# A linear-attention and feed-forward layer: x's loads behind K's reads, the residual's bias on VectorE, one normalisation later on ScalarE

## The reference

```
q, k, v = x @ Wq.T + bq, x @ Wk.T + bk, x @ Wv.T + bv     # cut into heads
q, k    = exp(q), exp(k)
kv, k1  = cumsum over tokens of k (outer) v, cumsum over tokens of k
att     = (q . kv) / (q . k1)                             # per head and token
x1      = layernorm(x + att @ Wo.T + bo)
h       = x1 @ weight @ aux_weight1 @ aux_weight2
out     = layernorm(x1 + tanh(h + bias))
```

## Time and profile before

| | us |
|---|---|
| median of 3 runs | 2340.22 (2339.27 to 2342.91) |
| the profiled execution | 2341.11, of it the traced span 2339.2 |

### The profile page before, as it was taken

The page is one execution under the profiler, slowest core; times in us unless marked ns, Lnnn a source line. Parts: engine busy times, 40 slices in busy tenths (PEclk is TensorE's granted clock), DMA queues, the critical chain, the costliest instruction groups (busy, mean ns, idle before and its releaser), DMA issues.

```text
span 2339.2 us, 71230 instructions
## 1 busy us (share of the span) xinstructions
PE 2249.3 (96%) x27784; PEld 1834.5 (78%) x27784; DVE 1494.7 (64%) x2316; ACT 1004.2 (43%) x1683; POOL 1415.9 (61%) x1925
## 2 busy tenths in 40 slices
PE   3999999999999999999999999999999999999985
PEld 2778888888888888888888888888888888878863
DVE  3466676666666766666667666676676666666653
ACT  2344444444444444444444444444444444444432
POOL 1256666666666666666666666666666666666563
PEclk9999999999999999999999999999999999999997
DMA  5133333333333333333333333333333333333221
GB/s 155 48 96 112 107 109 111 103 110 109 106 113 100 113 110 101 110 109 106 113 101 110 114 100 113 106 108 111 103 110 111 101 114 105 107 108 101 71 67 50
DMA packets 294452, 242.73 MB, mean 104 GB/s; under 512 B 33328, under 2 KB 225840, under 8 KB 294192
## 3 DMA queue, kind: packets, MB, share of 16 engines
q1 hardware_dynamic: 294192, 238.69, 32.6%
HBM read 139.99 MB, written 98.57 MB: 102 GB/s over the span
## 4 chain that ended last, share of the span: by engine, by line
PE 92%; DVE 2%; issue 2%; SPq 1%; DMA 1%; ACT 1%; POOL 1%; POOLq 0%; DVEq 0%; ACTq 0%
PE SC L312 25%; PE SC L313 24%; PE SC L314 24%; PE SC L410 6%; PE ND L419 5%; PE ND L397 3%; PE ND L393 2%; PE ND L429 2%; DVE o L684 1%; SPq L277 1%; DMA xres<-x 0%; PE ND L312 0%; PE ND L314 0%; DVE WK L654 0%; PE ND L313 0%
## 5 line engine op out<-in xcount | busy, mean ns | idle before, releaser
L723 POOL TENSOR_SCALAR_AFFINE_SELECT A<-A 128x512 f32<-128x512 f32 x512 | 329.3, 678 | 297.3 <-ACT A L532 297.2
L684 DVE RECIPROCAL o<-ND 128x512 f32<-128x512 f32 x128 | 427.8, 3342 | 1.6 <-PE ND L419 1.3
L700 DVE TENSOR_TENSOR xres<-SC,xres 128x512 f32<-128x512 f32 x128 | 88.5, 692 | 483.2 <-PE SC L314 358.0
L734 POOL TENSOR_TENSOR oL<-o,oH 128x512 fp32r<-128x512 f32 x128 | 165.3, 1291 | 325.0 <-ACT oH L542 325.0
L522 ACT ACTIVATE WK<-xres,shift,rstd 128x512 f32<-128x512 f32 x128 | 104.1, 813 | 501.5 <-POOL shift L770 501.5
L532 ACT ACTIVATE A<-SC 128x512 f32<-128x512 f32 x512 | 264.3, 602 | 36.0 <-PE SC L410 35.0
L312 PE MATMUL SC<-xTH,WqH 128*128 128x512 f32 x512 | 211.1, 412 | 32.3 <-POOL xTL L761 27.6
L312 PE MATMUL SC<-WoH,oH 128*128 128x512 f32 x512 | 202.4, 395 | 17.8 <-issue 16.5
L761 POOL TENSOR_TENSOR xTL<-xin,xTH 128x512 fp32r<-128x512 f32 x128 | 165.6, 1294 | 85.9 <-ACT xTH L567 85.9
L654 DVE TENSOR_TENSOR_SCAN WK<-ones,k,KT 128x128 f32<-128x128 f32 x512 | 207.6, 467 | 8.8 <-PE ND L393 8.3
L312 PE MATMUL SC<-WfH,x1H 128*128 128x512 f32 x512 | 201.0, 393 | 10.4 <-POOL x1L L748 9.4
(11 more groups left out here) (100 smaller groups left out, 5006.0 us busy)
## 6 DMA issues: line engine op xcount, KB each, us to landing
xin<-x SPq DMA_DIRECT2D x512, 64.0 KB, 2.0
xres<-x SPq DMA_DIRECT2D x128, 256.0 KB, 2.6
x_rows<-WK SPq DMA_DIRECT2D x128, 256.0 KB, 2.6
WK<-x_rows SPq DMA_DIRECT2D x512, 64.0 KB, 1.9
out<-WK SPq DMA_DIRECT2D x128, 256.0 KB, 2.0
k_rows<-WK SPq DMA_DIRECT2D x120, 256.0 KB, 2.0
WK<-k_rows SPq DMA_DIRECT2D x480, 64.0 KB, 1.9
QT<-wqT SPq DMA_DIRECT2D x4, 256.0 KB, 4.8
```

The lines of the kernel that those rows point to most:

```text
L684: nc.vector.reciprocal(o[:, :, :], den_ps).then_inc(recip_ready, 1)
L723: last = nc.gpsimd.affine_select(out=A[:, k % 2, j, :, :], in_=A[:, k % 2, j, :, :], compare_op=ALU.is_ge, fill=0.0, base=0, pattern=[[0, ...
L734: nc.gpsimd.tensor_tensor(oL[:, :, :], o[:, :, :], oH[:, :, :].bitcast(F32), ALU.subtract).then_inc(ol_ready, 1)
```

## The change

It moves three steps and touches no buffer. On SyncE the four loads of x's tile k+9 go behind the reads of x1 and K. The residual's bias is added on VectorE, in the slot in which the sum is made and right ahead of it, and no longer on GpSimd a slot earlier. On ScalarE the result's normalisation goes behind V's copy and x's split.

```
@@ -269,13 +269,6 @@
                     n = k - 1
                     wait_before(sp, (k_turned, c.count(n + 1)))
                     sp.dma_start(k_rows, KS).then_inc(k_stored[n % B], 16)
-                if c.exists(k + 9):
-                    n = k + 9
-
-                    wait_before(sp, (xl_ready, c.count(n - 1)))
-                    for j in range(HG):
-                        sp.dma_start(xin[j * HD:(j + 1) * HD, n % XIN, :].rearrange("p (t f) -> p t f", t=HG),
-                                     x_b[n % B, c.it + n // B, j]).then_inc(xin_loaded[n % B], 16)
                 if c.exists(k - 2):
                     n = k - 2
 
@@ -289,6 +282,13 @@
                     for j in range(HG):
                         sp.dma_start(Ktok[j * HD:(j + 1) * HD, :].rearrange("p (a c) -> p a c", a=HG),
                                      k_blocks[j]).then_inc(ktok_loaded[n % B], 16)
+                if c.exists(k + 9):
+                    n = k + 9
+
+                    wait_before(sp, (xl_ready, c.count(n - 1)))
+                    for j in range(HG):
+                        sp.dma_start(xin[j * HD:(j + 1) * HD, n % XIN, :].rearrange("p (t f) -> p t f", t=HG),
+                                     x_b[n % B, c.it + n // B, j]).then_inc(xin_loaded[n % B], 16)
                 if c.exists(k):
                     if c.static() and c.it * B + k == 0:
                         sp.wait_ge(c_done, 1)
@@ -551,11 +551,6 @@
                     wait(act, k_turned, c.quad_count(k - 4))
                     nc.scalar.activation(KT[:, ns, b, :], kproj_ps, ACT.Exp,
                                          bias=bcol[:, 1, b:b + 1]).then_inc(k_ready, 1)
-                if fin:
-                    n = k - 3
-                    wait(act, shift2_ready, c.count(n + 1))
-                    nc.scalar.activation(y[:, n % 2, :], y[:, n % 2, :], ACT.Identity, bias=shift[:, 1:2],
-                                         scale=rstd[:, 1:2]).then_inc(out_ready, 1)
                 if att:
                     wait(act, v_done, c.count(k + 1))
                     wait(act, state_done, c.state_count(k - 1))
@@ -568,6 +563,11 @@
                         xTH[:, (k // QUAD) % 2, :, b * P:(b + 1) * P].rearrange("p g (t q) -> p g t q", q=HD),
                         xin[:, k % XIN, :].rearrange("p (t g q) -> p g t q", t=HG, q=HD),
                         ACT.Copy).then_inc(xh_ready, 1)
+                if fin:
+                    n = k - 3
+                    wait(act, shift2_ready, c.count(n + 1))
+                    nc.scalar.activation(y[:, n % 2, :], y[:, n % 2, :], ACT.Identity, bias=shift[:, 1:2],
+                                         scale=rstd[:, 1:2]).then_inc(out_ready, 1)
 
             run_slots(act, slot, 8, 3, {-7: split_wq, -5: split_wk, -4: split_aux, -3: split_a12,
                                         -2: split_wv_wf_wo, -1: free_staging})
@@ -695,6 +695,8 @@
                     wait(dve, x1s_loaded[n % B], c.part_count(n))
                     nc.vector.transpose(x1s[:, :], x1s[:, :]).then_inc(x1_turned, 1)
                 if prev:
+                    wait(dve, xres_loaded[(k - 1) % B], c.dma_count(k - 1))
+                    nc.vector.tensor_tensor(r, r, cbc[:, :], ALU.add).then_inc(xb_ready, 1)
                     wait(dve, oproj_done, c.count(k))
                     wait(dve, xb_ready, c.count(k))
                     nc.vector.tensor_tensor(r, oproj_ps, r, ALU.add).then_inc(r_ready, 1)
@@ -747,12 +749,6 @@
                     halves = [t[:, :, :].rearrange("p g (t q) -> p g t q", q=HD) for t in (x1H, x1L)]
                     nc.gpsimd.tensor_tensor(halves[1], x1s[:, :].rearrange("p (t g q) -> p g t q", t=HG, q=HD),
                                             halves[0].bitcast(F32), ALU.subtract).then_inc(x1l_ready, 1)
-                if att:
-                    if not prev:
-                        pool.wait_ge(c_ready, 1)
-                    wait(pool, xres_loaded[k], c.dma_count(k))
-                    nc.gpsimd.tensor_tensor(xres[:, k % 2, :], xres[:, k % 2, :], cbc[:, :],
-                                            ALU.add).then_inc(xb_ready, 1)
                 if c.exists(k + 8):
                     m = k + 8
                     xs, cols = (m // QUAD) % 2, slice(m % QUAD * P, (m % QUAD + 1) * P)
```

More of the change, by code:

```diff
@@ L271, in slot @@
                     sp.dma_start(k_rows, KS).then_inc(k_stored[n % B], 16)
[L272 to L278, removed]
                 if c.exists(k - 2):
@@ L553, in slot @@
                                          bias=bcol[:, 1, b:b + 1]).then_inc(k_ready, 1)
[L554 to L558, removed]
                 if att:
@@ L749, in slot @@
                                             halves[0].bitcast(F32), ALU.subtract).then_inc(x1l_ready, 1)
[L750 to L755, removed]
                 if c.exists(k + 8):
```

## The result

| | us |
|---|---|
| before | 2340.22 (2339.27 to 2342.91) |
| after, median of 5 runs | 2354.84 (2350.71 to 2359.99) |
| ratio | 1.006 [1.0047, 1.0073] |
| the profiled execution after | 2359.99, of it the traced span 2358.2 |

The forecast was 2337.7, in a range of 2334 to 2343. The kernel became slower by 14.6 us, and the forecast was wrong. The profiled execution is the slowest of the five; its span is 19.0 us longer than that of before, so what follows sizes about 19 us where the medians differ by 14.6.

What follows compares the result with a forecast made beforehand. TensorE was taken to bound the kernel, with 11.4 us of disturbances the most to gain. Gains of 0.9 us (SyncE's order) and 1.6 us (bias move), ScalarE's order 0, took 2340.22 to 2337.7 us, range 2334 to 2343.

Steps and rivals of the forecast that it cites:

- What bounds the kernel: TensorE bounds the steady stretch: undisturbed slots last 17.24 us, and all disturbances over 112 slots are 11.4 us.
- the unnamed 5 us of disturbances: TensorE, steady stretch: the remaining 5 us or so of 11.4 are later starts not counted as idle.
- Part 1: SyncE's order: reads of x1 start 3.1 us earlier in slot 53, L696's 1.34 us wait goes; gain at most 0.9 us.
- The gain of 0.9 us: TensorE's waits ahead of the feed-forward in slots 113 and 115 go, at most 0.41 and 0.5 us.
- rival A: Nothing arrives at TensorE: late slots had other causes too, or other slots become late instead; 2340.2 us, chance 0.25.
- Part 2: Residual's bias from GpSimd to VectorE: removes TensorE's waits for L532, gain 1.6 us; addition takes 0.69 us at cost 0.
- three waits for L532: TensorE's Q product waits three times for ScalarE's copy of the scores; all should go, 1.6 us.
- Part 3: ScalarE's order: V's copy and x's split no longer wait behind the normalisation, result's store up to 1.2 us later; worth 0.
- The sum: Whole kernel: 0.9 + 1.6 = 2.5 us gained, so a median of 2337.7 us.
- last sign: Forecast is wrong if an undisturbed slot isn't 17.24 us or disturbances over 112 slots grow beyond 11.4 us.
- D: SyncE's reads don't get earlier because x1's store lands later beside K's; 2338.6 us, chance 0.58 together with the forecast.
- C: VectorE's addition stops GpSimd for its whole length, x1L 0.14 us late in each of 112 slots; 2356 us, chance 0.07.

Runs made afterwards that it cites:

- e2: Kernel before with only SyncE's new order (x's loads behind the reads of x1 and K); 2347.57 us, ratio 1.0032.
- e4: Kernel before with SyncE's new order and the residual's bias on VectorE, ScalarE's order unchanged; 2344.19 us, ratio 1.0015.
- e10: Kernel before with SyncE's new order and the bias addition on VectorE right behind the quotient (L686), ScalarE's order unchanged; 2341.72 us, ratio 0.9996.
- e1: Kernel before with only ScalarE's new order (result's normalisation behind V's copy and x's split); 2342.92 us, ratio 1.0011.
- e11: Kernel before with ScalarE's new order and one needless one-column GpSimd instruction ahead of x1L, bias still on GpSimd; 2359.16 us, ratio 1.0064.
- e7: Kernel before with ScalarE's new order and the bias on VectorE, SyncE's order unchanged; 2354.70 us, ratio 1.0064.
- e9: Kernel after with the addition L699 moved directly behind the quotient L686, where GpSimd has nothing to do; 2345.88 us, ratio 1.0012.
- e12: Kernel of e9 with GpSimd's x1L ahead of the second normalisation's scale and shift; 2340.91 us, ratio 0.9994.
- e3: Kernel before with only the residual's bias moved from GpSimd to VectorE; 2344.47 us, ratio 1.0017.
- e6: Kernel after with the result's store issued a slot later, ahead of the residual's load; 2342.54 us, ratio 1.0013.

## Why the prediction was wrong

**What bounds the kernel** held: TensorE does, and an undisturbed slot is 17.24 us in both kernels. But I listed the L429 waits "with no releaser" and the unnamed 5 us of disturbances and didn't ask what they were. More than half of all the 11.4 us is waits for the program. In before, TensorE's starts that come over 0.13 us late add up to 10.3 us in slots 9 to 120; of these 6.5 us, in 17 places at L429, L313 and once L393, come 1.3 to 1.5 us after a block's landing. In after it is 27.8 of 29.6 us, counting distances of 1.1 to 1.8 us.

**Part 1** was right in its mechanism. In slot 53 of after the reads of x1 start 2.92 us behind its store. SyncE's timeline, to be read against the earlier trace rows:

```profile
1011.78 0.33 SPq L267 DMA_DIRECT2D x_rows<-WK  x1
1014.70 2.83 SPq L277 DMA_DIRECT2D WK<-x_rows  x4
1021.74 0.35 SPq L296 DMA_DIRECT2D xres<-x  x1
1024.30 0.37 SPq L300 DMA_DIRECT2D out<-WK  x1
```

VectorE's wait of L696 for `x_rows` fell from 98.0 us to 9.3. One statement failed, "The residual's load stays about where it was": in the median of a place in the loop pass it moved by up to 0.9 us in e2 and up to 1.3 us in after. That cost 0.32% in e2 and was free beside part 2 (e4). The gain of 0.9 us came where it was forecast: slots 113 and 115, 18.08 and 17.95 us before, are 17.24 in after. But slot 114, 17.24 before, takes 18.33 in after and 18.34 in e10, so it was taken back next door, as rival A had it. In e10, with both parts in a harmless form, the time can't tell (0.9996, with 2.5 us inside the interval).

**Part 2.** The gain is there in kind: GpSimd's L761 waits for VectorE's statistics nearly always, so that GpSimd is no longer the late one, and one of three waits for L532 is left (1.6 us before, 1.0 after). Waits of after, whole span:

```profile
POOL ve L761 <- DVE mv L706: 231.0, 127, 4.2
DVE WK L696 <- DMA WK<-x_rows: 9.3, 13, 2.7
```

The step that failed is "GpSimd's list can be stretched [...] x1L still comes 0.93 - 0.38 = 0.55 us early. Cost 0". The stretch was right in size: x1L came 0.33 us later, and in slot 63 still 0.73 us ahead of its product. What failed is that I measured its spare time at the product alone. The fetch of the next block of TensorE's program follows x1L too, and for that second user less than 0.3 us was to spare once the store was in the way (e1 against e11). The duration failed too: 0.69 us was taken for L699 between 0.69 and 1.07, and it took 1.146 on average, above both ends. The 1.07 us of slot 1 was no ceiling: there the product started with 0.53 us left of GpSimd's mask (L723) and ended 0.54 us after it. Beside oL 0.65 us were left, and the same 0.54 us on top give the longer time. The row to read was how much of GpSimd's work is left when the addition starts. VectorE's idle time covered that, as the text said: L702 still waits for TensorE, 3.51 us in slot 53 of after.

**Part 3** failed at "The result's store is issued up to about 1.2 us later [...] 0". It was 0.76 us later, and the only question put was who wants its buffer. Whose transfers it meets was not asked. Alone it cost 0.11% (e1), about as little as I said; together with the addition it cost 0.64% (e7).

**The sum** was made of terms that were taken one by one. Its own last sign fired: the disturbances grew from 11.4 to 31.0 us while the undisturbed slot stayed at 17.24. The three parts alone give 0.11 + 0.32 + 0.17 = 0.60%, which happens to be the change's 0.6%; but e4 (0.15%) is far below its two parts and e7 (0.64%) far above, so the agreement is an accident of one healing and one harmful pair.

**The rivals.** A and D were nearest to the forecast. Neither time came, though A was right that other slots become late in place of 113 and 115. C had the price by accident (2356) and the right pair of engines, but not the path: in it x1L is late for its product from 0.93 us on, whereas the loss began at 0.3 us and at another place. With 0.07 for anything slower, the lack was a rival for what moves in time beside TensorE: two transfers that used to pass each other by.

## What to carry to other kernels

Before an edit that shifts a large transfer by less than a microsecond is priced at nothing, look at what else starts there in the view of transfers, the instruction queue included. If TensorE waits with no releaser at the same place of each loop pass, suspect its program's blocks, and look whether one landed 1.2 to 1.5 us before TensorE resumed. Spare time has to be read for every user of a signal, and the fetch of TensorE's program is one of them. And parts of a change that are harmless alone have to be timed in pairs.

## What the runs showed of the hardware

- TensorE's program of a loop pass arrives in 15 transfers of 16 KB, and TensorE, when it stood waiting for one at a turn of after, resumed 1.2 to 1.5 us after it had landed (24 cases). At the turn of the loop one such transfer that starts or lands about 1 us late made the next slot 1.6 us longer (17.42 to 19.00 in the median). An instruction of 0.21 us on another engine decided it (e11).
- Among the packets of a store of 256 KB such a transfer takes longer: 1.51 us in the median in e7, 1.35 in e1, 1.00 before.
- An addition of two SBUF tiles on VectorE that starts during a GpSimd subtraction of two SBUF tiles is held up until that ends: 1146 against 680 ns (after and e9). A `tensor_scalar` of one column on GpSimd that is due during the addition is held up in turn: 537 against 232 ns. In the one slot of after where the addition started 0.06 us ahead of the subtraction, it took 650 ns and the subtraction 1744 instead of 1297. The Trainium skill, "GPSIMD Engine Reference", Specifications, names this contention; these runs agree with it.
- What stays open: what besides x1L sets the start of the fetch (e12), why e3 to e6 keep some 0.15% although their turns are nearly quiet, what delays the fetch in 4 turns of e6, and the part of before's 11.4 us that is no wait for a block. None of the twelve kernels is shown to be faster than before: every interval reaches above 1.
